# ScalarE loads its table and W1 of MLP block one ahead of the first turned rows; VectorE copies turned rows ahead of the bias, in a macaron layer with a mixture of experts

## What is computed

```
x = x + 0.5 * ffn(layernorm(x), ...)      # first MoE
x = x + attention_layer(layernorm(x), ...)
x = x + 0.5 * ffn(layernorm(x), ...)      # second MoE

def ffn(x):                                # 8 experts, the best 2 for each row
    w_full = top-2 of softmax(x @ gate_W), normalized
    # experts 0 to 3: an MLP, 128 -> 512 -> 128
    h = gelu(x @ mlp_W1[e] + mlp_b1[e]);  mlp_out = h @ mlp_W2[e] + mlp_b2[e]
    # experts 4 to 7: a KAN, 8 hills for each input, 128*8 -> 256, then 256*8 -> 128
    h0 = layernorm(x) * g0 + b0;  basis0 = 1 - tanh((h0 - grid) / 2)**2
    z = basis0 @ kan_W0[e] + kan_b0[e]
    h1 = layernorm(z) * g1 + b1;  basis1 = 1 - tanh((h1 - grid) / 2)**2
    kan_out = basis1 @ kan_W1[e] + kan_b1[e]
    out = sum over e of expert_out[e] * w_full[e]
```

## Time and profile before

| | |
|---|---|
| median of three executions | 686.47 us |
| the profiled execution | 683.25 us, span 681.4 us |
| TensorE matmul busy | 541.8 us (80%) |
| TensorE weight load busy | 471.3 us (69%) |
| VectorE busy | 450.6 us (66%) |
| ScalarE busy | 373.8 us (55%) |
| GpSimd busy | 263.2 us (39%) |
| mean granted TensorE clock | 0.90 |

### The profile page before, as it was taken

How to read it: one execution, slowest core, us unless ns; L and a number is a source line. 1 busy time by engine, 2 the same in 40 slices (tenths; PEclk the granted TensorE clock), 3 DMA queues, 4 the chain that set the end, 5 groups by cost and what they waited for, 6 DMA issues and landing times. The chain is left out here.

```text
span 681.4 us, 18347 instructions
## 1 busy us (share of the span) xinstructions
PE 541.8 (80%) x6060; PEld 471.3 (69%) x6061; DVE 450.6 (66%) x1166; ACT 373.8 (55%) x876; POOL 263.2 (39%) x305
## 2 busy tenths in 40 slices
PE   5358999999997287786999939973389899999970
PEld 4247899999986244564788835662378899999960
DVE  5743878878877495997133384558338688777855
ACT  2326889888944036401565512232268798888930
POOL 6035466666544246700000020120354566666530
PEclk9999999999999779857899978965589999999985
DMA  9962222110100400000000000069610001001106
GB/s 250 381 266 69 66 66 70 31 31 27 24 15 16 132 1 3 2 13 2 15 4 4 5 0 1 1 191 322 264 36 20 27 27 31 28 27 29 24 16 189
DMA packets 41235, 46.51 MB, mean 68 GB/s; under 512 B 7216, under 2 KB 33184, under 8 KB 40160
## 3 DMA queue, kind: packets, MB, share of 16 engines
q1 hardware_dynamic: 32224, 34.00, 15.4%
q0 software_dynamic: 4736, 9.71, 5.4%
q10 hardware_dynamic: 4224, 2.10, 1.0%
HBM read 35.69 MB, written 10.09 MB: 67 GB/s over the span
## 5 line engine op out<-in xcount | busy, mean ns | idle before, releaser
L845 PE MATMUL k_y_ps<-kan_w,k_basis 128*128 x1056 | 127.4, 280 | 8.2 <-DVE k_basis L941 6.5
L845 PEld LDWEIGHTS k_y_ps<-kan_w,k_basis 128*128 128x128 f32 x1056 | 123.9, 196 | 10.0 <-issue 9.9
L835 PE MATMUL k_z_ps<-kan_w,k_basis 128*128 x528 | 119.9, 380 | 1.0 <-issue 1.0
L1106 ACT ACTIVATE k_sig<-k_h1T 128x256 f32<-128x256 f32 x264 | 84.5, 402 | 53.2 <-DVE k_h1T L966 53.0
L835 PEld LDWEIGHTS k_z_ps<-kan_w,k_basis 128*128 128x128 f32 x528 | 97.7, 190 | 13.8 <-issue 1.5
L941 DVE SCALAR_TENSOR_TENSOR k_basis<-k_sig 128x512 f32<-128x512 f32 x132 | 85.8, 691 | 15.7 <-ACT k_sig L1106 15.7
L1099 ACT ACTIVATE k_sig<-k_h0T 128x128 f32<-128x128 f32 x280 | 59.2, 293 | 0.0
L1668 ACT ACTIVATE got<-p_ps 128x960 f32<-128x960 f32 (+1 forms) x44 | 39.2, 944 | 28.0 <-PE p_ps L1584 28.0
L661 POOL DMA_INDIRECT y_rows<-k_y,k_rows x33 | 33.2, 1005 | 50.4 <-DVE k_y L973 32.5
L1632 DVE TENSOR_REDUCE p_minus_max<-p_ps 128x6 f32<-128x960 f32 (+1 forms) x44 | 46.1, 1120 | 6.6 <-PE p_ps L1549 4.9
L813 PE MATMUL m_z_ps<-m_xT,m_w 128*128 128x128 f32 x304 | 46.0, 300 | 4.3 <-DVE m_xT L979 3.1
(11 more groups left out here) (252 smaller groups left out, 1017.5 us busy)
## 6 DMA issues: line engine op xcount, KB each, us to landing
kan_w<-in_L_ffn_kan_sl_W_dram SPq DMA_DIRECT2D x16, 1024.0 KB, 10.3
x_rows<-got SPq DMA_DIRECT2D x4, 1024.0 KB, 12.4
mlp_w<-in_L_ffn_mlp_W_dram SPq DMA_DIRECT2D x2, 1024.0 KB, 5.8
mlp_w<-in_L_ffn_mlp_W_dram SPq DMA_DIRECT2D x8, 256.0 KB, 6.6
got<-y_rows SPq DMA_DIRECT2D x8, 256.0 KB, 4.9
got<-y_rows ACTq DMA_DIRECT2D x8, 256.0 KB, 5.4
xs<-in_L_attn_x_dram SPq DMA_DIRECT2D x4, 256.0 KB, 3.5
s_cos<-in_cos_dram SPq DMA_DIRECT2D x8, 128.0 KB
```

Of the source, the lines that this page charges most:

```text
L835: last = nc.tensor.matmul(z_ps, basis0[:, g], k.kan_w0[:, bass.ds(e, 1), g], start=(g == 0), stop=(g == G - 1))
L845: last = nc.tensor.matmul(y_ps, basis1[:, g, c], k.kan_w1[:, bass.ds(e, 1), c, g], start=(g == 0 and c == 0), stop=(g == G - 1 and c == F2 ...
L1106: ins = nc.scalar.activation(sig1[:, g], h1T[:], ACT.Sigmoid, bias=float(-GRID[g]))
```

## The change

Three edits, each in `moe_blocks`, so each acts twice.

1. ScalarE loads the Sigmoid table first of all, then waits for the MLP weights, reads the experts and copies W1 of block 1 without a wait for turn 1. The eight sigmoids of the first KAN block move ahead of W1 of block 2.
2. VectorE reads the experts of the first KAN and MLP blocks ahead of its first `m_copy`, not behind it.
3. In the pair loop VectorE does `m_copy(j + 2)` ahead of `m_take_z(j + 1)`, not behind it.

```diff
@@ VectorE, start
+                e_first = kan_experts(dve, 1, 4)
+                e_mlp = mlp_experts(dve, 1, 1)[0]
                 m_copy(1)
-                e_first = kan_experts(dve, 1, 4)
                 affine0(0, e_first[0])
-                m_take_z(first, mlp_experts(dve, 1, 1)[0])
+                m_take_z(first, e_mlp)
                 m_copy(2)
                 hills0(0, 0)
                 hills0(0, 1)
@@ VectorE, pair loop
                         j = 2 * ii + (1 + u)
+                        m_copy(j + 2)
                         m_take_z(j + 1, e_pair[u + 1])
-                        m_copy(j + 2)
                         dve.wait_ge(m_y_free, j)
                         m_take_y(j, m_y[u], e_pair[u])
@@ ScalarE
                 def m_take_w1(j, e):
-                    act.wait_ge(m_turned, j)
+                    if j is not first:
+                        act.wait_ge(m_turned, j)
                     nc.scalar.copy(m_w1[:], k.mlp_w1[:, bass.ds(e, 1)].rearrange("p o f -> p (o f)")
                                    ).then_inc(m_w1_ready, 1)
@@ ScalarE, start
+                act.preload_act_table(ACT.Sigmoid)
                 act.wait_ge(k.mlp_loaded[n], 16 * N_MLP)
                 _, *e_first = mlp_experts(act, 0, 5)
-                m_take_w1(1, e_first[0])
-                act.preload_act_table(ACT.Sigmoid)
+                m_take_w1(first, e_first[0])
                 note_rows(1, 0)
                 note_rows(2, 1)
+                sigmoids0(0)
                 m_take_w1(2, e_first[1])
-                sigmoids0(0)
                 act.preload_act_table(ACT.Gelu)
                 gelu(first)
                 m_take_w1(3, e_first[2])
```

## The result

The changed kernel takes 683.18 us, the median of 20 runs (680.95 to 685.98). The kernel before takes 685.89 us in 20 runs beside them (682.03 to 688.23). The ratio is 0.9964 with a 95% interval of 0.995 to 0.9978, so 2.5 us are gained (0.0036 x 685.9), with an interval of 1.5 to 3.4; the medians alone differ by 2.7. The forecast was 683.1 and a gain of 3.4.

What follows compares the result with a forecast made beforehand. ScalarE's queue between turn 1 and the first Gelu was taken to bound the stretch ahead of a full joint loop. Terms -1.72 - 1.40 + 0.2 - 0.5 = -3.4 us took 686.47 to 683.1, range 681.3 to 685.2.

Steps and rivals of the forecast that it cites:

- First MoE, gain of 1.72: First MoE, W2 matmuls of block 1: start at 51.35 instead of 53.07, behind turn 3 rather than Gelu.
- The inner steps: First MoE, before the W2 matmuls: first W1 matmuls 0.32 earlier, at 46.02; sigmoids from 46.45 to 48.15.
- Second MoE, gain of 1.40: Second MoE, W2 matmuls of block 1: start at 494.58 instead of 495.98, with KAN rows coming late.
- The three chains that were to meet within 0.1 us: Second MoE, ahead of the first W2 matmuls: W1 of block 2 at 492.5, Gelu 494.55, turn 494.58.
- Edit 3, loss of 0.2: Pair loop, copy ahead of bias: 2 x 0.1 us lost; bounds a gain of up to 0.28, a loss of 0.4.
- The clock, 0.5: TensorE, early steps of both MoEs: clock rises earlier with the gap closed, 0.5 us gained; bounds 1.56 lost, 1.8 gained.
- The sum, 3.4: Whole kernel: -1.72 - 1.40 + 0.2 - 0.5 = -3.4 us, from 686.47 to 683.1.
- The profiled execution, 679.8: The one profiled execution of the whole kernel: 683.25 would become 679.8 us.
- One gap stays: One MoE: `h0T` or a table load comes late, only 1.4 to 1.7 gained, 684.9 us; chance 0.10.
- Swallowed: Behind the start, GpSimd's gathers and scatters: a later turn waits, no change, 686.5 us; chance 0.09 together with the queue blocking.
- The queue blocks: Pair loop, VectorE: bias behind a waiting copy, 3.2 lost against 3.6 gained, 686.1 us; chance 0.09 together with swallowing.
- Slower by a late clock: Early steps of both MoEs: clock rises only after the pair loop, 8.8 lost against 2.9 gained, 692.4 us; chance 0.05.

Runs made afterwards that it cites:

- e10: Kernel before with only the loop counts held at 1 or more, run again on a third chip: 684.46 us, ratio 1.0 to before.
- e9: All three edits plus loop counts held at 1 or more, run again on the third chip: 680.45 us, ratio 0.9943 to before.
- e1: All three edits plus loop counts held at 1 or more, on the first chip: 683.15 us, ratio 0.9959 to before.
- e6: All edits, loop counts held, but W1 of block 2 ahead of the sigmoids again: 687.56 us, ratio 1.0019 to before.
- e7: All edits, loop counts held, but Sigmoid load and W1 of block 1 behind turn 1 again: 686.4 us, ratio 1.0007 to before.
- e0: Kernel before with only the loop counts held at 1 or more, on the first chip: 687.27 us, ratio 1.0012 to before.
- e11: Edits 1 and 2 without edit 3 (bias ahead of copy), loop counts held, third chip: 678.93 us, ratio 0.9921 to before; 6 runs.
- e4: Edits 1 and 3 without edit 2 (expert reads behind VectorE's first copy), loop counts held: 687.3 us, one run.
- e8: All edits, loop counts held, plus identity matmuls ahead of the wait for the first rows: 681.89 us, ratio 0.9968 to before.

## Why the prediction was right, and where it wasn't

**First MoE, gain of 1.72: right.** From the KAN turn 7.73 became 5.97 at the same gap of 0.27, so 1.76; between e10 and e9 it is 1.62, or 7.99 - 6.24 = 1.75 from turn 1, since their gaps differ. The forecast 51.35 was made for a turn at 45.34. The turn came 1.16 later, and 51.35 + 1.16 = 52.51 stands against 52.47. The inner steps hold too: sigmoids 1.06 behind the KAN turn (predicted 46.45 - 45.34 = 1.11), W1 matmuls 0.68 behind it after 1.00 before, so 0.32 earlier.

**Second MoE, gain of 1.40: right, for the late KAN rows that it assumed.** The forecast put the W2 matmuls 494.58 - 489.04 = 5.54 behind the KAN turn; e1 and e9, with gaps of 1.31 and 1.16, have 5.54, and 6.94 - 5.54 = 1.40. In the profile of the changed kernel the gap was 0.62 and not 1.44, so its 6.94 - 5.62 = 1.32 compares two cases; a kernel without the edits would have started them 8.0 behind turn 1 there, and this one did 6.24 behind it. The size of the gain depends on the gap, which the prediction took as fixed in each MoE. The three chains that were to meet within 0.1 us did so harmlessly: Gelu ends at 493.33 + 0.63 = 493.96, turn 3 starts at 494.09 and the W2 matmuls 0.21 behind it.

**What carries it: shown at the W2 matmuls.** e6 takes the order of the sigmoids back, and there 1.41 of the 1.76 goes in the first MoE and all of the gain in the second. e7 takes the early load back and about half goes, with early KAN rows in both MoEs. The two act together, as ScalarE's sum of durations said. That the time follows is shown by e1 and e9 against e0 and e10; for e6 and e7 it rests on a comparison across chips. That edit 2 was needed was only argued.

**Edit 3, loss of 0.2: undecided.** Bias rows do stand behind copy rows. Ahead of the W1 matmuls of blocks 4 and 5 TensorE waits 1.15 + 0.83 and 1.01 + 0.62 us in e9, and 0.97 + 0.70 and 0.59 + 0.27 in e11, so 1.08 more with the edit. But the three groups ahead of these waits are 0.9 shorter in e9, by an earlier clock, and from the W2 to the KAN matmuls the edit costs -0.08 and 0.39. That is what I had bounded, and the timed pairs can't give the sign.

**The clock, 0.5: the step that was borne out at most in part.** The rise did come forward. I had put it 1.25 and 2.0 us behind the first W2 matmuls; it came at 53.5 and 497.2, so 1.0 and 2.9 behind, where it had been 3.3 and 4.2. (In the first MoE these instants are worked out from the durations of the groups: the windows of before and after give 1.00 there from 44 us on, although eight matmul records last 2.04 us, as they do at 0.50 in the second MoE.) The first W2 group lasts 1.55 in the first MoE (predicted saving 0.4, measured 2.07 - 1.55 = 0.52) and 1.92 in the second. But little of it is handed on: from the W2 matmuls to the KAN matmuls e10 takes 10.74 and 10.63 us, e9 10.67 and 10.66. The clock and edit 3 were to give 0.3 together, and gave 0.04 in these profiles. e11, which has the earlier rise without edit 3, takes 10.75 and 10.27, so 0.35 less than e10, and by the same reading edit 3 costs 0.31: one profile each, which can't rule out that the two terms stood as forecast and cancelled. The rows of e10 and e9 show where it goes. The W2 matmuls of blocks 1 and 2 and W1 of block 3 take 5.06 and 5.19 us in e10 and 3.82 and 4.41 in e9, so the clock saves 2.0. W1 of block 3 alone is 1.92 and 1.41 in the second MoE. Then TensorE waits 0.33 + 0.51 and 0.15 + 0.69 ahead of W1 of blocks 4 and 5 in e10, and 1.15 + 0.83 and 1.01 + 0.62 in e9, so 1.9 more. Those waits end with VectorE's rows, with W1 from ScalarE and with TensorE's own issue: the pair loop there goes at the pace of the other engines. I had reckoned with that for one group of the first MoE only. Why the timed pairs show 4.0 and not 3.1 stays open.

The Trainium skill (TensorE: Matmul & The Clock Gate, part 1) lets the rise follow sustained activity in time and not a number of matmuls. The traces agree as far as they go: with the standstill closed the rise moved from 3.3 and 4.2 to 1.0 and 2.9 us behind the first W2 matmuls. They don't tell time from number.

**The sum, 3.4: inside the interval.** The comparison gives 2.5 (1.5 to 3.4), the two pairs of experiments 4.1 and 4.0, and the two MoEs measured by themselves 3.1. The carrying over from 683.25 to the median was a guess that mattered little: the median of before came out at 685.89 in 20 runs, not 686.47, and this slip of 0.6 made up for most of a gain forecast 0.7 too high by the medians (0.9 by the ratio). The match of 683.1 with 683.18 is luck, closer than the reasoning.

**The profiled execution, 679.8: wrong by 3.1.** It took 682.9. The first rows came 1.16 us later, and in its pair loops two signals came late. The W2 matmuls of block 3 end at 58.21 + 1.06 = 59.27 by the profile, and both readers of that signal start 1.9 to 2.1 us later: Gelu 4 at 61.15 and `m_take_y` at 61.32, both put down to "remote" above. In the second MoE they end at 501.52, and Gelu starts at 502.58. In e9 the same matmuls end at 57.82 and `m_take_y` starts at 58.03. So this one profile shows a gain at the KAN matmuls of only 0.67 + 0.71 = 1.4 us.

**The rivals.** One gap stays: e7 shows that it can happen, where rows land at other times, but not with the early load. Swallowed: excluded by the time of e9 against e10 and of e1 against e0. The queue blocks: nothing like its 3.2 us is seen, though e9 has the 1.08 more of waits named above. Slower by a late clock: the clock rose earlier, not later, but the fear had a grain of truth, told below.

## What to carry to other kernels

Where one engine's queue sets the start of a pipeline, list its operations by when their inputs can be there at the earliest, and put those without inputs (a table load, a copy of a weight) into the wait ahead; then order the others by who waits for them, not by block number. Measure such a change from an instruction that it can't move to one well behind it, since executions of one kernel differ by twice the gain. If that start itself varies, as with two gathers here that land 0.3 to 1.4 us apart, compare executions in which it was the same. And test the order by itself: here one pair of lines decides over nearly the whole gain at the W2 matmuls.

## What the runs showed of the hardware

**The clock falls again soon after it has risen.** Windows of e1 in the first MoE:

```profile
57.00:60.70 3.70, 1.77 (x16) 1.61 (x16) 1.18 (x3) 1.25 (x3) 1.72 (x2) 1.00 0.26 73
60.70:64.10 3.40, 3.40 (x19) 3.40 (x18) 0.89 (x2) 0.88 (x4) 2.18 (x3) 0.50 0.26 77
```

TensorE was busy 1.77 of 3.70 us, at a granted clock of 1.00; then the clock is 0.50 for 3.40 us in which TensorE is busy throughout, and from 64.1 on it is 1.00 again. W1 of block 5 takes 1.76 us there instead of 1.13. Falls at 64.7 and 64.9 us are in the profiles of e0 (without any edit) and e4, one at 507.6, as the KAN matmuls of the second MoE begin, in that of e7, and that of e8 was shown above; before, after, e9, e10 and e11 have the clock at 1.00 from 56 to 68 us. So it comes with and without the edits. As groups take 2.04 us at the lower level and 1.13 at the higher, 3.4 busy us at half speed cost about 1.5 to 1.7 us by my estimate, over half of what the change gains. In the twelve timed runs of e9 the time goes with the mean granted clock: the four with 0.904 to 0.906 took 676.0 to 677.9 us, the eight with 0.897 to 0.901 took 679.5 to 682.9. e1 reaches the KAN matmuls 2.12 us later than e9 in the first MoE, in part by this and in part by the late signals told next.

**Signals of matmuls that come late.** Delays like those told above, up to 2.3 us and put down to "remote", are in the profiles of the changed kernel and of e1 to e7, on the first two chips, and in none of before, e0 and e8 to e11. e8, e9 and e11 have the edits without them, so the change alone doesn't bring them; but every profile that shows them has at least one edit, and e0 is the only kernel without an edit that was profiled on those chips. (Gelu of block 4 is late in e0 too, 1.90 us behind the end of the W2 matmuls of block 3, but there it stands on ScalarE behind W1 of block 5, 63.39 + 0.62, and that behind row numbers that had waited 1.92 us for a store.) Whether the change has a part in them is therefore open, as are their cause and whether the timed runs have them. The Trainium skill (Perfetto Trace Analysis, "Tensor Engine Instruction (MATMUL, LD_WEIGHTS)") says that the recorded end of a matmul is computed and that the semaphore follows only when all bytes are written. By that rule a part of these 2 us may lie in the matmuls; no run here can divide it.
